# Decoder layer on one core: the next element's queries and keys projected ahead of the later self-attention scores, through one PSUM bank, with their stacking transfers behind the last of these scores

## What is computed

```python
x = layernorm(x + self_attention(x))          # causal, 16 heads of 16, bias on qkv and projection
x = layernorm(x + cross_attention(x, ctx))    # 16 heads of 64, 77 context tokens
x = layernorm(x + ffn(x))                     # +-1 weights: [x,-x] -> 1024 -> 1024 -> 256, relu between
```

## Time and profile before

| | us |
|---|---|
| median of 3 runs | 2592.23 |
| lowest, highest | 2591.71, 2593.98 |
| the profiled execution's own time | 2591.91 |
| its span, first to last instruction | 2590.2 |
| PE busy | 2198.6 (85%) |
| DVE busy | 1471.9 (57%) |
| ACT busy | 1134.2 (44%) |
| POOL busy | 683.8 (26%) |
| transfers of q1, share of 16 engines | 36.4% |

### The profile page before, as it was taken

One profiled execution on the slowest core, in us unless ns is written; L12 is line 12 of the kernel. 1 busy time (PEld: TensorE's weight loads), 2 busy tenths in 40 slices (PEclk: granted clock), 3 DMA queues, 4 the chain that ended last, 5 costly groups with the idle time before them and its releaser, 6 DMA issues.

```text
span 2590.2 us, 54551 instructions
## 1 busy us (share of the span) xinstructions
PE 2198.6 (85%) x18572; PEld 1907.4 (74%) x18572; DVE 1471.9 (57%) x4548; ACT 1134.2 (44%) x2568; POOL 683.8 (26%) x847
## 2 busy tenths in 40 slices
PE   7995578988888888888888888888988888888897
PEld 6884467877777777777777777777877777777776
DVE  4542355655565665566556555656655665555564
ACT  5552334444444444444444444444444444444443
POOL 1000223223222322322322232223233223222321
PEclk9997689999999999999999999999999999999999
DMA  8885333223323333332233233333223323333310
GB/s 271 277 277 142 62 63 67 56 53 55 61 42 60 65 65 65 65 59 53 55 57 55 47 65 65 65 65 65 52 51 61 61 38 65 65 65 65 65 38 9
DMA packets 205156, 196.58 MB, mean 76 GB/s; under 512 B 50130, under 2 KB 184306, under 8 KB 205042
## 3 DMA queue, kind: packets, MB, share of 16 engines
q1 hardware_dynamic: 205108, 195.94, 36.4%
HBM read 69.37 MB, written 58.87 MB: 50 GB/s over the span
## 4 chain that ended last, share of the span: by engine, by line
PE 62%; DMA 11%; DVE 9%; issue 7%; SPq 5%; ACT 5%; DVEq 1%; POOL 0%; POOLq 0%; ACTq 0%
DMA k_bd<-p2t 9%; PE ps L1312 9%; PE ps L1143 9%; PE ps L1183 5%; PE ps L1184 5%; PE ps L1166 4%; PE ps L1280 4%; PE ps L1219 4%; PE ps L1232 4%; SPq L393 3%; PE ps L1208 2%; PE ps L1124 2%; PE ps L1132 2%; DVE junk L826 2%; PE ps L1207 2%
## 5 line engine op out<-in xcount | busy, mean ns | idle before, releaser
L1183 PE MATMUL ps<-r_h,w 128*128 128x256 f16 x2048 | 497.2, 285 | 1.9 <-DVE r_l L812 1.9
L1184 PE MATMUL ps<-r_l,w 128*128 128x256 f16 x2048 | 493.3, 283 | 0.0
L826 DVE CUSTOM_DVE_ANT_0 junk<-ps,causal 128x128 bf16<-128x128 f32 (+1 forms) x1024 | 328.2, 355 | 177.6 <-PE ps L1208 174.1
L490 POOL TENSOR_TENSOR p<-p2r,inv 128x308 f32<-128x308 f32 x256 | 194.7, 779 | 584.5 <-DVE inv L876 579.4
L601 ACT ACTIVATE p2r<-ps,low 128x77 f32<-128x77 f32 x1024 | 247.5, 343 | 118.3 <-DVE low L865 118.2
L1207 PE MATMUL ps<-k_bd,q_st 128*128 128x256 f32 x256 | 95.7, 374 | 225.9 <-DMA k_bd<-p2t 202.4
L565 ACT ACTIVATE r_h<-ps 128x512 f16<-128x512 f32 x256 | 152.6, 596 | 275.8 <-PE ps L1184 268.3
L476 POOL TENSOR_SCALAR_AFFINE_SELECT probs<-probs 128x512 f32<-128x512 f32 x256 | 164.0, 641 | 375.1 <-ACT probs L626 371.9
L1312 PE MATMUL ps<-vo_h,p2t 128*128 128x256 f32 (+1 forms) x1280 | 234.5, 290 | 24.6 <-DVE p2t L883 24.6
L812 DVE SCALAR_TENSOR_TENSOR r_l<-ps,r_h 128x512 f16<-128x512 f32 x256 | 176.1, 688 | 131.7 <-ACT r_h L565 131.7
L1280 PE MATMUL ps<-k_bd,q 128*128 128x154 f32 x1024 | 174.4, 302 | 79.4 <-ACT p2r L601 79.4
(11 more groups left out here) (145 smaller groups left out, 4948.2 us busy)
## 6 DMA issues: line engine op xcount, KB each, us to landing
vo_scratch<-vo_out SPq DMA_DIRECT2D x80, 448.0 KB, 4.6
vo<-vo_scratch SPq DMA_DIRECT2D x64, 512.0 KB
q_st<-p2t SPq DMA_DIRECT2D x192, 128.0 KB
k_bd<-p2t SPq DMA_DIRECT2D x192, 128.0 KB, 6.8
q<-q SPq DMA_DIRECT2D x128, 128.0 KB, 2.1
k_bd<-k_scratch SPq DMA_DIRECT2D x64, 154.0 KB, 3.4
x_in<-in_x SPq DMA_DIRECT2D x32, 256.0 KB, 5.4
out<-y SPq DMA_DIRECT2D x32, 256.0 KB, 6.8
```

What stands on the lines that cost most here:

```text
L490: pool.tensor_tensor(unit_probs(t), raw, inv.unsqueeze(3).to_broadcast([P, TB, 2, SK]), ALU.mult)\
L826: dve.tensor_tensor_reduce(out=junk[:, e, b * P:b * P + width], in0=ps[:, 2 + b, e * width:(e + 1) * width], in1=causal[:, (1 - b) * P:], ...
L1183: pe.matmul(dst, w1[:, kk, m * P:(m + 1) * P], r0_h[:, kk, :], start=kk == 0, stop=False)
L1184: last = pe.matmul(dst, w1[:, kk, m * P:(m + 1) * P], r0_l[:, kk, :], start=False, stop=kk == KF - 1)
```

## The change

- TensorE: the x transposes of `i + 1` move from behind values 2 to behind the transposed maxima of `i`; the query projection moves in front of scores by key 4, the key projection in front of scores 7. Scores 7 come ahead of block 1 of layer 0. The values projection stays where it was.
- One bank: x transposes, queries, keys and values projection all go through bank 3, each waiting until ScalarE and VectorE have read the one before. All `values` of an element now use bank 2, with a wait for ScalarE's copy before `values` 2.
- SyncE: the load of the next `x` goes first. `head_stacks` is split: `query_stacks` waits for the last scores by key and goes between packing 0 and packing 1; `key_stacks` goes behind packing 1.
- ScalarE and VectorE follow: their reads of x, queries and keys move forward, and on ScalarE `self_probs` 7 ahead of the first relu.
- Cross stage: `self_max` of the next scores 0 moves ahead of the low part of transposed `x1`, `self_max` 3 from unit 4 to unit 5, and two blocks of layer 1 move from between cross scores 6, 7 and the transposes to behind the transposes and into the later group of blocks.

```diff
@@ -376,8 +376,10 @@
...
-    def head_stacks(j):
...
+    def query_stacks(j):
...
+        if not (isinstance(j, int) and j == 0):
+            sp.wait_ge(pe_st, nth(j, NP, 0))
         sp.wait_ge(a_qk, nth(j, 4, 2))
@@ -387,6 +389,9 @@
...
+    def key_stacks(j):
@@ -404,23 +409,28 @@
...
+    def output_packed(i, m):
+        sp.wait_ge(a_o, nth(i, 2, m + 1))
+        sp.dma_start(s_c[:, m, :], o_raw[1::2, 2 * m:2 * m + 2, :]).then_inc(s_packed[m], 16)
+        sp.dma_start(o_c[:, m, :], o_raw[0::2, 2 * m:2 * m + 2, :]).then_inc(o_packed[m], 16)
...
     def attention(i, g, first=False, more=True):
+        if more:
+            load(i + 1)
         if not first:
...
         load_value_outputs(i)
-        if more:
-            load(i + 1)
         stack_max(i, 1)
-        for m in range(KD):
-            sp.wait_ge(a_o, nth(i, 2, m + 1))
-            sp.dma_start(s_c[:, m, :], o_raw[1::2, 2 * m:2 * m + 2, :]).then_inc(s_packed[m], 16)
-            sp.dma_start(o_c[:, m, :], o_raw[0::2, 2 * m:2 * m + 2, :]).then_inc(o_packed[m], 16)
-        if more:
-            head_stacks(i + 1)
+        output_packed(i, 0)
+        if more:
+            query_stacks(i + 1)
+        output_packed(i, 1)
+        if more:
+            key_stacks(i + 1)
         if g is not None:
@@ -431,7 +441,8 @@
...
-    head_stacks(0)
+    query_stacks(0)
+    key_stacks(0)
     stack_max(0, 0)
@@ -566,13 +577,13 @@
     def transposed_x(j):
         act.wait_ge(pe_xt, nth(j, 1, 1))
-        act.activation(xt_h[:], ps[:, 4, :], ACT.Copy).then_inc(a_xt, 1)
+        act.activation(xt_h[:], ps[:, 3, :], ACT.Copy).then_inc(a_xt, 1)
     def queries_keys(j, u):
...
         for m in (2 * u, 2 * u + 1):
-            act.activation(qk_h[:, m, :], ps[:, 6 + u, (m % 2) * S:(m % 2 + 1) * S], ACT.Identity,
+            act.activation(qk_h[:, m, :], ps[:, 3, (m % 2) * S:(m % 2 + 1) * S], ACT.Identity,
                            bias=bias_qk[:, m:m + 1]).then_inc(a_qk, 1)
@@ -628,7 +639,7 @@
     def self_output(i, m):
         act.wait_ge(pe_pv, nth(i, 4, 2 * m + 2))
-        act.activation(o_raw[:, 2 * m:2 * m + 2, :], ps[:, 2 + m, :], ACT.Copy).then_inc(a_o, 1)
+        act.activation(o_raw[:, 2 * m:2 * m + 2, :], ps[:, 2, :], ACT.Copy).then_inc(a_o, 1)
@@ -640,29 +651,28 @@
...
         self_probs(i, 3)
+        if more:
+            transposed_x(i + 1)
         if not first:
...
         self_probs(i, 4)
+        if more:
+            queries_keys(i + 1, 0)
         self_probs(i, 5)
...
         self_probs(i, 6)
+        if more:
+            queries_keys(i + 1, 1)
+        self_probs(i, 7)
         if not first:
             relu(0, r0_h, pe_z0, a_r0, f, 0)
-        self_probs(i, 7)
-        if more:
-            transposed_x(i + 1)
         self_output(i, 1)
...
             relu(0, r0_h, pe_z0, a_r0, f, 2)
-        if more:
-            queries_keys(i + 1, 0)
-        if not first:
             relu(1, r0_h, pe_z0, a_r0, f, 3)
-        if more:
-            queries_keys(i + 1, 1)
         self_output_high(i, 1)
@@ -831,19 +841,19 @@
     def transposed_x(j):
         dve.wait_ge(a_xt, nth(j, 1, 1))
-        dve.tensor_tensor(xt_l[:].rearrange("p a b -> p (a b)"), ps[:, 4, :],
+        dve.tensor_tensor(xt_l[:].rearrange("p a b -> p (a b)"), ps[:, 3, :],
                           xt_h[:].rearrange("p a b -> p (a b)").bitcast(F32), ALU.subtract).then_inc(d_xt, 1)
     def queries_keys(j, m):
         dve.wait_ge(a_qk, nth(j, 4, 2 * (m // 2) + 2))
-        dve.scalar_tensor_tensor(qk_l[:, m, :], ps[:, 6 + m // 2, (m % 2) * S:(m % 2 + 1) * S],
+        dve.scalar_tensor_tensor(qk_l[:, m, :], ps[:, 3, (m % 2) * S:(m % 2 + 1) * S],
                                  bias_qk[:, m:m + 1], qk_h[:, m, :].bitcast(F32),
...
     def self_values(j):
         dve.wait_ge(pe_v, nth(j, 1, 1))
-        dve.tensor_tensor(v[:, :, :, 0::2], ps[:, 5, :].rearrange("p (b h d) -> p b h d", b=TB, d=HD),
+        dve.tensor_tensor(v[:, :, :, 0::2], ps[:, 3, :].rearrange("p (b h d) -> p b h d", b=TB, d=HD),
                           bias_v[:].rearrange("p (h d) -> p h d", d=HD).unsqueeze(1).to_broadcast([P, TB, H, HD]),
@@ -891,16 +901,23 @@
...
             ffn_sum(g, 0)
-        if not first:
-            transposed_x2(f)
+        if more:
+            transposed_x(i + 1)
         if g is not None:
             ffn_sum(g, 1)
+        if not first:
+            transposed_x2(f)
+        if more:
+            queries_keys(i + 1, 0)
+            queries_keys(i + 1, 1)
+        if g is not None:
             layer_norm_stats(2, y3, g)
+        if more:
+            queries_keys(i + 1, 2)
+            queries_keys(i + 1, 3)
         if not first:
...
         self_output(i, 0)
-        if more:
-            transposed_x(i + 1)
         if not first:
@@ -911,8 +928,6 @@
...
         if more:
-            for m in range(4):
-                queries_keys(i + 1, m)
             self_values(i + 1)
@@ -925,11 +940,11 @@
...
         layer_norm_apply(0, x1, x1, d_x1, i)
+        if more:
+            self_max(i + 1, 0)
         dve.wait_ge(a_x1t, nth(i, 1, 1))
...
                           xt_h[:].rearrange("p a b -> p (a b)").bitcast(F32), ALU.subtract).then_inc(d_x1t, 1)
-        if more:
-            self_max(i + 1, 0)
         if not first:
@@ -941,8 +956,8 @@
...
             cross_sum(i, t - 1)
-            if t in (2, 4) and more:
-                self_max(i + 1, 1 + t // 2)
+            if t in (2, 5) and more:
+                self_max(i + 1, 2 + t // 4)
             if t == KX - 2:
@@ -1225,31 +1240,39 @@
...
             pe.wait_ge(a_nm, nth(i, 2, 2))
+        if g == 2:
+            pe.wait_ge(a_o, nth(i, 2, 1))
         c = (g % 2) * S
...
                 src = pr[:, (2 * g + j // 2) % 4, j % 2, (1 - b) * P:(3 - 2 * b) * P]
-                last = pe.matmul(ps[32 * j:32 * j + 32, 2 + g // 2, c + b * P:c + S], v[:, b, 4 * g + j, :], src,
+                last = pe.matmul(ps[32 * j:32 * j + 32, 2, c + b * P:c + S], v[:, b, 4 * g + j, :], src,
                                  start=b == 0, stop=b == 1)
...
     def transposed_inputs(j):
         pe.wait_ge(x_loaded, nth(j, 16, 16))
-        transposes(x_in, 4, j, pe_xt)
+        transposes(x_in, 3, j, pe_xt)
     def queries_keys(j, u):
+        if u == 0:
+            pe.wait_ge(a_xt, nth(j, 1, 1))
+            pe.wait_ge(d_xt, nth(j, 1, 1))
+        else:
+            pe.wait_ge(d_qk, nth(j, 4, 2))
         for m in (2 * u, 2 * u + 1):
-            last = weights_by_tokens(ps[:, 6 + m // 2, (m % 2) * S:(m % 2 + 1) * S], wqkv_h, wqkv_l,
+            last = weights_by_tokens(ps[:, 3, (m % 2) * S:(m % 2 + 1) * S], wqkv_h, wqkv_l,
                                      slice(m * P, (m + 1) * P), xt_h, xt_l)
...
     def self_values(j):
+        pe.wait_ge(d_qk, nth(j, 4, 4))
         for b in range(TB):
-            last = tokens_by_weights(ps[:, 5, b * D:(b + 1) * D], xt_h, xt_l, b, wqkv_h, wqkv_l,
+            last = tokens_by_weights(ps[:, 3, b * D:(b + 1) * D], xt_h, xt_l, b, wqkv_h, wqkv_l,
                                      slice(2 * D, 3 * D))
@@ -1345,6 +1368,8 @@
...
         transposed_max(i, 1)
+        if more:
+            transposed_inputs(i + 1)
         filler2(2)
@@ -1352,33 +1377,28 @@
...
             transposed_x2(f)
+        if more:
+            queries_keys(i + 1, 0)
         scores_by_key(i, 4)
...
         scores_by_key(i, 6)
+        if more:
+            queries_keys(i + 1, 1)
+        scores_by_key(i, 7)
         filler0(1)
-        scores_by_key(i, 7)
         values(i, 2)
-        if more:
-            pe.wait_ge(a_p, nth(i, NP, NP - 1))
-            transposed_inputs(i + 1)
         if g is not None:
...
         filler0(5)
-        if more:
-            pe.wait_ge(a_xt, nth(i + 1, 1, 1))
-            pe.wait_ge(d_xt, nth(i + 1, 1, 1))
-            queries_keys(i + 1, 0)
         filler0(6)
...
         if more:
-            queries_keys(i + 1, 1)
             self_values(i + 1)
@@ -1389,6 +1409,7 @@
...
         if more:
+            pe.wait_ge(d_v, nth(i + 1, 1, 1))
             pe.wait_ge(q_stacked, nth(i + 1, 112, 112))
@@ -1398,9 +1419,6 @@
...
         pe.wait_ge(k2_loaded, nth(i, 32, 32))
-        if more:
-            pe.wait_ge(d_qk, nth(i + 1, 4, 4))
-            pe.wait_ge(d_v, nth(i + 1, 1, 1))
         def next_scores(n):
@@ -1420,12 +1438,10 @@
...
         cross_scores(i, 6)
-        layer1_until(f, 17, 18)
         cross_scores(i, 7)
-        layer1_until(f, 18, 19)
         cross_transposes(i, 0, 0)
         cross_transposes(i, 0, 1)
-        layer1_until(f, 19, 22)
+        layer1_until(f, 17, 20)
         cross_output(i, 0, 0)
@@ -1433,7 +1449,7 @@
...
         cross_transposes(i, 1, 1)
-        layer1_until(f, 22, 24)
+        layer1_until(f, 20, 24)
         cross_output(i, 1, 0)
@@ -1462,11 +1478,10 @@
...
     pe.wait_ge(w_low[3], 1)
-    pe.wait_ge(a_xt, 1)
-    pe.wait_ge(d_xt, 1)
     queries_keys(0, 0)
...
     self_values(0)
+    pe.wait_ge(d_v, 1)
```

(11 more changed lines are left out.)

2 lines of the change are left out of this document (1 added, 1 removed).

## The result

The changed kernel takes 2477.11 us in the median of 4 runs (2476.13 to 2479.52), the kernel before 2592.45. The ratio is 0.9556 with a 95% interval of 0.9539 to 0.9572: faster by 4.4%. The profiled execution took 2479.52 us, its span is 2477.8, 112.4 us less than before. The forecast was 2488.

A forecast was written before the change was run, and what follows sets the result against it. Bound: TensorE's first score by query waiting for late key stacks. 5.76 + 1.9 + 0.3 − 0.4 − 1.6 − 3.4 − 1.3 + 2.1 = 3.35 us, times 31: 104 us off 2591.9, 2488 us; 80% range 2395 to 2550.

The forecast's parts named there:

- old wait for the stacks, gone: TensorE's first score by query would no longer wait for the last key-stack transfer, saving 5.76 us an iteration.
- half clock behind the old wait, gone: TensorE's work at 1.2 instead of 2.4 GHz after the key-stack wait would disappear, saving 1.9 us an iteration.
- wait at layer 0: TensorE would idle 1.6 us before layer 0's seventh block, for VectorE's relu_low 1; ends 0.5 and 2.2.
- wait at layer 1: TensorE would idle 3.4 us at layer 1's fourth block, for relu_low behind packing and reciprocal; ends 0 and 5.
- half clock behind the wait at layer 1: After the layer 1 idle time the clock would fall in most iterations, costing 1.3 us; bounds 0 and 1.9.
- scores by key, idle time gone: Scores by key would no longer wait for the stacked maxima, saving 0.3 us an iteration.
- cross stage, waits gone: Cross scores 7 would start earlier and moved layer-1 blocks cover a 0.74 us wait: 2.1 us saved; ends 1.2 and 2.6.
- each microsecond would be one: At TensorE's x transposes: if x came later than 1210.2, each microsecond late would cost one microsecond.
- Packing through at once: Rival: packing lands at T + 6.7, layer 1 waits 0.8 us, clock stays full; 2398 us, chance 0.14.
- Larger backlog: Rival: packing lands at T + 11.3, layer 1 idles 5 us, clock falls for 1.9 us; 2553 us, chance 0.12.
- Doesn't do what it says: Rival: stacks still end last, T moves little, only the cross stage's 2.1 us remain; 2527 us, chance 0.07.
- The slower case: Rival: packing behind query stacks makes VectorE's second reciprocal wait longer than the wait removed; 2665 us, chance 0.07.

The follow-up runs named there:

- The filled wait: The changed kernel with 28 idle matmuls added ahead of the fourth block of layer 1, where TensorE waits for relu_low; 2433.6 us, ratio 0.9384.

## Why the prediction was right

**The sum, point by point.** Times on the prediction's clock and waits, in microseconds. The last column is the mean over the 29 iterations of the loop, with waits read from 400 to 2470 us before and from 400 to 2360 us after.

| step | predicted | iteration shown | loop |
|---|---|---|---|
| start of the stacks | 1220.5 | 1220.6 | |
| reciprocal begins | 1229.9 | 1230.0 | |
| last key transfer there | 1236.9 | 1237.3 | |
| old wait for the stacks, gone | 5.76 | 5.76 | 5.91 |
| half clock behind the old wait, gone | 1.9 | 1.9 | 1.9 |
| wait of the key projection for the bank | 0.4 | 0.35 | 0.34 |
| wait at layer 0 | 1.6 | 1.10 | 1.10 |
| wait at layer 1 | 3.4 | 3.53 | 3.49 |
| half clock behind the wait at layer 1 | 1.3 | 1.7 | 1.6 |
| scores by key, idle time gone | 0.3 | | 0.07 |
| cross stage, waits gone | 2.1 | 2.15 | 2.1 |
| all in an iteration | 3.35 | 3.38 | 3.67 |

The step that carried it was to look for what the moved transfers were put in front of, and to price the packing by the backlog and not by its median of 2.1 us. The packing between the query transfers showed that it is that backlog: two transfers less, 2 us less.

**Terms that were mis-sized, and partly cancel.** The wait at layer 0 was put 0.5 us too high, the half clock 0.3 too low. The 0.3 us for scores by key was wrongly read: the 10.0 us of the page were spread over all elements, but only 2.1 of them lie in the loop, the rest in the first 400 us. The terms of the last column make 3.45; 0.2 us of the 3.67 stay without a place. That 3.35 comes so near to the 3.38 of the iteration shown is in part luck.

**Clock.** That a wait of 3.4 us would bring the half clock back "in most iterations" held, in 27 of 29. The filled wait measured its price apart, 1.4 us over 31 iterations, and the neighbouring iterations 1.7 for one fall.

**Cross stage.** 2.1 us predicted, 1.9 measured on the kernel before, 2.8 on top of the moved stacks. The mechanism is shown by the rows: cross scores 7 waited 1.57 and wait 0.16. The moved stacks give 28 us alone and 55 with the other part, and by the estimate from TensorE's busy time most of that difference is half clock.

**Where the other microseconds were won.** Predicted were 104 us, measured 112.4 of span. The first scores by query for the elements 2 and 31 bound the 29 iterations of the loop, before:

```profile
379.96 0.55 PE L1207 MATMUL ps<-k_bd,q_st 128*128 128x256 f32 x1 [5.85 <-DMA k_bd<-p2t]
...
2458.31 0.58 PE L1207 MATMUL ps<-k_bd,q_st 128*128 128x256 f32 x1 [6.07 <-DMA k_bd<-p2t]
```

and after:

```profile
376.76 0.36 PE L1222 MATMUL ps<-k_bd,q_st 128*128 128x256 f32 x1
...
2348.63 0.36 PE L1222 MATMUL ps<-k_bd,q_st 128*128 128x256 f32 x1
```

That is 71.67 us an iteration before and 68.00 after: 3.67 won, 106.5 us in all. The pair of iterations compared above (71.58 and 68.20) gives 0.3 us less than the mean. The opening lost 3.1 us, not 1: the first score by query of all moved from 248.34 to 251.46. The two iterations in front of the loop won 6.3 us and the end of the span 2.7. So the term that was too small is the 3.35 us of an iteration, and by 0.3 us only.

**What was costed at nothing** was the early load of `x`, hidden by scores and layer 2. That held with 2.7 us to landing. But "each microsecond would be one" was too low: 2.8 us late cost 4.4, since the wait brought a fall of the clock of its own.

**The rivals.** Packing through at once: no; it lands 4.9 us after its issue. Larger backlog: no, the first transfer of the pair lands 9.4 us and the second 10.1 us after the start of the stacks, where 9.8 was taken for the second. "Doesn't do what it says": no, the stacks start 3.4 us earlier. The slower case, the queue's second chain becoming a longer wait than the removed one, has its price shown by the neighbours in order: 2388.7, 2477.1 and 2585.4 us for the packing after four, after six and before all query transfers. The place of one pair of transfers in one queue is worth 197 us here.
